# Shared expert in blocks of 128 and 48 columns over whole groups, first x1 loads moved into the attention, and other engine orders, in a decoder layer on one core

## The chip, the core and the metric

The kernel runs on one core of a Trainium2 chip. The core has TensorE (PE, matrix products into eight PSUM banks), VectorE (DVE), ScalarE (ACT), GpSimd (POOL) and SyncE (SP, here only an issuer of DMAs). Each engine works through its own instructions in order, and they meet at semaphores. Sixteen DMA engines carry every transfer, whoever issues it. The metric is the device time of the whole program in microseconds, lower is better.

## What is computed

One decoder layer over 4096 tokens (64 sequences of 64) with 256 features, all in float32: a strided self attention, an attention over 64 context rows that keeps the 54 highest scores, and a mixture of 16 routed experts (4 per token) beside one shared expert. The change touches the shared expert and the gate:

```python
x = x + _L0_attn_ref(_layernorm(x, axis=-1), ...)
x = x + _L0_xattn_ref(_layernorm(x, axis=-1), ..., ctx_2048, ctx_2048, 54)
x = x + _L0_ffn_ref(_layernorm(x, axis=-1), ...)

# in the last one: D, H, NE = 256, 176, 16
logits = jnp.einsum('ed,btd->bte', gate_w, x)
scores = jax.nn.sigmoid(logits) + gate_b
weights, indices = jax.lax.top_k(scores, TOP_K)
weights = weights / weights.sum(-1, keepdims=True)
shared_out = jax.nn.silu(x @ w1_shared) * (x @ w3_shared) @ w2_shared
h1 = jnp.einsum('btd,edc->btec', x, w1_routed)
h2 = jnp.einsum('btd,edc->btec', x, w3_routed)
h3 = jax.nn.silu(h1 * h2)
experts_out = jnp.einsum('btec,ecd->bted', h3, w2_routed)
return shared_out + routed_out
```

## The kernel before

The program has three phases with a barrier of all engines between them.

**Attention** (`attention_phase`). Four blocks of 1024 tokens, eight steps each. SP loads the inputs, stores the result rows to the DRAM scratch `x1`, and, between the loads of the first two blocks, prefetches the small weights of the next phase (`CrossInputs.load`). DVE is busy nearly all the time.

**Cross phase** (`cross_phase`). Eight groups of 512 tokens go through a software pipeline. Round i does stage s of group i - s; each engine runs the pieces of a round in the order that the table `order` lists (t is TensorE, v VectorE, s ScalarE, g GpSimd). For group n:

- stage -1 and 0: statistics and normalisation of x1 (`stA`, `rsA`, `nmA`, `xhA`), transposition (`t_a`, `t_a_ev`), queries (`at_mm`, two halves, `at_ev`) and the value side (`bp_mm`, `bp_ev`);
- stage 1: scores (`sc_mm`), their mask on VectorE (`negs`, `tops`, `masks`) with the exponential `expo` on ScalarE, the transposed probabilities (`p_t`, moved from PSUM to SBUF by ScalarE in `p_t_ev`), the product with the values (`y_mm`), the residual `x2_`, then the statistics of x2 (`stC`, `rsC` on GpSimd, `nmC`, `xhC`);
- stage 2: transposition (`t_c`, `t_c_ev`), gate (`lg_mm`, `th_`, `l_t`), routing on VectorE (`choose`, `shares`, `spread`, which needs the ranks of `rk_mm` and writes `slot`, the place of each row), and the first eight of 16 scatters of the group: `scatter(0)` and `scatter(1)` on GpSimd, each an indirect DMA of 128 rows to `xs_scratch`;
- stage 3: the other eight scatters (`scatter(2)`, `scatter(3)`), and the shared expert in two halves of 256 tokens: `sh_mm`, `g1_` (Silu), `hs_`, `ys_mm`, `xf_`.

The two normalisations are tied to GpSimd: `rsA` and `rsC` take a power of four numbers per row, and stand between the scatters of the same engine. A scatter k waits until scatter k - 2 has landed (`s_sc`, two semaphores by turns), so at most two are in flight. GpSimd's order in a round is `rsA`, four scatters, `rsC`, four scatters, and then eight of the next group, which wait for its `slot`.

The hidden width is 176. Before, it is cut in two halves of 88 (`HC`): `sh_mm` has for each half of the tokens eight products of 256 columns for 88 outputs, and the gate is a product of its own with 16 outputs. A float32 product of up to 512 columns shows as two MATMUL rows in the trace and in the counts of the profile.

At the start of the phase ScalarE issues six DMAs with the routed weights (`load_weights`, 8.65 MB on queue q10), and only then computes the coefficients `cf` for which VectorE waits before its first statistics. SP issues the first three loads of x1 (`load_x1`, 512 KB each) at the same time; for later groups it issues x1, context and output DMAs round by round.

**Experts** (`expert_phase`). 143 tiles of 128 rows are gathered from `xs_scratch`, and each result is added to the output by an indirect DMA. It starts when every engine and every scatter of the cross phase is done. The change does not touch it.

## Time and profile before

| | us |
|---|---|
| runs without profile: median (lowest, highest) of 3 | 904.76 (896.44, 906.59) |
| the profiled execution, its own time | 898.93 |
| its span, first to last instruction | 896.8 |
| attention, until the barrier | 0 to 242 |
| cross phase | 242 to 545 |
| experts | 545 to 897 |

| engine | busy us | share of the span |
|---|---|---|
| PE | 700.3 | 78% |
| DVE | 596.4 | 67% |
| POOL | 529.8 | 59% |
| ACT | 393.7 | 44% |

Busy shares are means over three phases with different limits, so they don't say what a change in one phase is worth. For that one looks at a stretch of time, asks which engine goes on without a pause or waits only for itself, and follows who waits for whom. In a timeline row the number in square brackets is the idle time of the engine just before the row, with the engine and line that ended it. Line numbers L... are those of the kernel before.

### The profile page before, as it was taken

The page shows a single profiled execution, that of the slowest core. Times are in us where ns is not written, and L with a number is a line of the kernel's source. Part 1 is how long each engine was busy: PE and PEld are TensorE (multiplying, and loading weights), DVE is VectorE, ACT ScalarE, POOL GpSimd, SP SyncE. Part 2 cuts the span into 40 slices and gives each one's busy share as a digit, 9 for nine tenths or more (in the row PEclk, how much of TensorE's full clock was granted, in tenths as well). Part 3 has the DMA queues.
Part 4 walks back from the last instruction along what each step waited for, and adds up shares of the span by engine and source line. Part 5 has one row for each costly group of instructions (what it writes and reads, how often), then busy time and mean ns, then how long its engine had stood idle before and what let it go on. Part 6 is the DMA issues. An engine that isn't in the chain of part 4 may idle for free. (4 is left out here: it accounts for less than half of the span.)

```text
span 896.8 us, 19120 instructions
## 1 busy us (share of the span) xinstructions
PE 700.3 (78%) x4330; PEld 589.3 (66%) x4330; DVE 596.4 (67%) x1833; ACT 393.7 (44%) x1051; POOL 529.8 (59%) x419
## 2 busy tenths in 40 slices
PE   0777777775405799988997754999999999898993
PEld 0556665664303567655775433899999999898993
DVE  4799999999202666554564464777777777576672
ACT  0644435352003555444542233655555555454451
POOL 0587877776300036666567671667677756764875
PEclk9988979798856999998998885999999999999997
DMA  6701111000296224433223453567677767676874
GB/s 198 248 26 41 54 35 47 29 23 19 72 302 112 71 82 150 157 128 127 104 104 122 144 187 101 95 113 132 121 126 128 125 115 126 110 131 101 132 124 54
DMA packets 86893, 99.04 MB, mean 110 GB/s; under 512 B 10401, under 2 KB 81633, under 8 KB 86753
## 3 DMA queue, kind: packets, MB, share of 16 engines
q0 software_dynamic: 26736, 37.64, 23.2%
q1 hardware_dynamic: 48971, 51.68, 19.9%
q10 hardware_dynamic: 11094, 8.65, 4.1%
q8 instruction: 39, 0.64, 0.3%
q14 instruction: 53, 0.43, 0.2%
HBM read 49.57 MB, written 52.95 MB: 114 GB/s over the span
## 5 line engine op out<-in xcount | busy, mean ns | idle before, releaser
L1412 POOL DMA_INDIRECT out_dram<-yw,xg x143 | 223.3, 1561 | 127.0 <-issue 59.1
L1008 POOL DMA_INDIRECT xs_scratch<-rows,slot x128 | 128.2, 1002 | 78.7 <-DMA xs_scratch<-rows,slot 50.1
L1305 PE MATMUL cbank<-w,stc_hi 88*128 x572 | 116.0, 295 | 1.4 <-DVE stc_lo L1377 0.5
L1305 PE MATMUL cbank<-w_hi,xtc_hi 128*128 x286 | 106.5, 372 | 0.6 <-DVE xtc_lo L1317 0.3
L1305 PEld LDWEIGHTS cbank<-w,stc_hi 88*128 88x128 f32 x572 | 90.3, 190 | 14.3 <-issue 9.2
L1305 PE MATMUL cbank<-w,xtc_hi 128*128 x286 | 94.0, 329 | 0.0
L1305 PE MATMUL cbank<-w_hi,xtc_lo 128*128 x286 | 93.6, 327 | 0.0
L455 PE MATMUL ps_o<-ident,pv 128*128 128x128 f32 x288 | 48.6, 328 | 54.9 <-ACT ot L291 50.1
L1397 DVE TENSOR_SCALAR yw<-cbank,xg 128x256 f32<-128x256 f32 x143 | 69.0, 483 | 29.1 <-PE cbank L1305 16.3
L1317 DVE TENSOR_TENSOR xtc_lo<-cbank,xtc_hi 128x256 fp32r<-128x256 f32 x143 | 60.6, 423 | 36.9 <-ACT xtc_hi L1312 26.2
L455 PEld LDWEIGHTS ps_o<-ident,pv 128*128 128x128 f32 x288 | 40.4, 170 | 63.7 <-POOL pv L256 42.8
L1305 PE MATMUL cbank<-w,stc_lo 88*128 x286 | 80.9, 283 | 0.0
L1357 ACT ACTIVATE sgc<-hh 128x176 f32<-128x176 f32 x143 | 50.1, 350 | 63.6 <-DVE hh L1351 51.7
L1345 ACT ACTIVATE h<-cbank 128x176 f32<-128x176 f32 x143 | 45.2, 316 | 71.8 <-PE cbank L1305 56.0
L1294 PE MATMUL cbank<-identb,xg 128*128 128x128 f32 x286 | 56.5, 279 | 25.5 <-DMA xg<-xs_scratch 25.5
L256 POOL TENSOR_TENSOR pv<-v_sb,pr 128x256 f32<-128x256 f32 (+7 forms) x32 | 70.0, 2187 | 6.4 <-DVE pr L423 6.4
L1351 DVE TENSOR_TENSOR hh<-cbank,h 128x176 f32<-128x176 f32 x143 | 48.5, 339 | 29.9 <-ACT h L1345 22.5
L706 POOL TENSOR_TENSOR rstd<-ve,powerb 128x4 f32<-128x4 f32 x16 | 16.5, 1028 | 75.8 <-DVE ve L700 75.6
L1312 ACT ACTIVATE xtc_hi<-cbank 128x256 fp32r<-128x256 f32 x143 | 53.5, 374 | 13.9 <-PE cbank L1294 12.8
L1377 DVE TENSOR_TENSOR stc_lo<-cbank,stc_hi 88x256 fp32r<-88x256 f32 x143 | 58.7, 410 | 1.0 <-ACT stc_hi L1372 0.9
L1305 PEld LDWEIGHTS cbank<-w_hi,xtc_hi 128*128 128x128 f32 x286 | 55.2, 193 | 2.4 <-issue 1.6
L1305 PEld LDWEIGHTS cbank<-w,xtc_hi 128*128 128x128 f32 x286 | 55.5, 194 | 0.0
(191 smaller groups left out, 1722.8 us busy)
## 6 DMA issues: line engine op xcount, KB each, us to landing
xg<-xs_scratch SPq DMA_DIRECT2D x143, 144.0 KB
x_in<-x_dram SPq DMA_DIRECT2D x32, 128.0 KB
w_hi<-ctx_t_dram SPq DMA_DIRECT2D x8, 512.0 KB, 3.6
x_scratch<-u SPq DMA_DIRECT2D x32, 128.0 KB
w_hi<-x_scratch SPq DMA_DIRECT2D x8, 512.0 KB
out_dram<-w SPq DMA_DIRECT2D x16, 256.0 KB
w<-w1r_dram ACTq DMA_DIRECT2D x2, 1408.0 KB
w<-w3r_dram ACTq DMA_DIRECT2D x2, 1408.0 KB
```

What stands on the lines that cost most here:

```text
L256: f_pv.sig(e.tensor_tensor(pv[:, p % 2, 0:w, :].rearrange("p b (h d) -> p b h d", h=H), v_sb[:, gg % 2, 0:w, :].rearrange("p b (h d) -> p ...
L455: last = e.matmul(ps_o[:, ch * P:(ch + 1) * P], pv[:, p % 2, b, ch * P:(ch + 1) * P], ident[:, :], is_transpose=True, start=b == 0, stop=b ...
L1008: nc.gpsimd.indirect_dma_start(t["xs"], bass.IndirectOffsetOnAxis(ap=slot[:, n % 2, k:k + 1].bitcast(U32), axis=0), rows[:, n % NROW, k // ...
L1294: last = nc.tensor.transpose(R[p % 2][:, ch * P:(ch + 1) * P], xg[:, p, ch * P:(ch + 1) * P], ident[:, :])
L1305: last = nc.tensor.matmul(out, stationary, moving, start=j == 0, stop=j == len(pairs) - 1)
L1312: f["t_hi"].sig(nc.scalar.activation(xt_hi[:, p % 2, :, :], x_t(p), ACT.Copy))
L1317: f["t_ev"].sig(nc.vector.tensor_tensor(xt_lo[:, p % 2, :, :], x_t(p), xt_hi[:, p % 2, :, :].bitcast(F32), ALU.subtract))
L1351: f["hh"].sig(nc.vector.tensor_tensor(hh[:, p % 2, :], R[2 + p % 2][:, 0:HID], h2[:, p % 2, :], ALU.mult))
L1357: f["sg"].sig(nc.scalar.activation(sg[:, p % 2, :], hh[:, p % 2, :], ACT.Silu))
L1377: f["st_ev"].sig(nc.vector.tensor_tensor(st_lo[:, p % 2, :, :], s_tr(p), st_hi[:, p % 2, :, :].bitcast(F32), ALU.subtract))
L1397: f["y_ev"].sig(nc.vector.tensor_scalar(yw[:, p % YB, :], R[6 + p % 2][:, 0:D], xg[:, p, bass.ds(c, 1)], None, ALU.mult))
L1412: nc.gpsimd.indirect_dma_start(t["out"], bass.IndirectOffsetOnAxis(ap=xg[:, p, ID:ID + 1].bitcast(U32), axis=0), yw[:, p % YB, :], None, c ...
```

## The change

1. **Shared expert in 128 and 48 columns, whole groups.** `sh_mm` now does all 512 tokens of a group at once with the first 128 of 176 columns: w1 into bank 2, w3 into bank 3, two products of 512 columns each. The remaining 48 columns of w1 and w3 and the 16 of the gate stand in one block `wrest` of 128 columns (48 of w3, 16 zeros, 48 of w1, 16 gate), and `rest_mm` takes the place of `lg_mm`. So the rest is computed in stage 2 (`g1r_`, `hsr_`) and the main part in stage 3 (`g1_`, `hs_`). `ys_mm` adds 128 rows of `w2s` and 48 of `w2rest`, its second half into bank 3 instead of bank 2.
2. **First x1 loads in the attention.** The three loads of x1 for groups 0 to 2 are issued by SP in the attention, after the last input loads, behind a wait for the stores of block 1 and ahead of the stores of blocks 2 and 3.
3. **Other engine orders** in `order` for TensorE, VectorE and ScalarE. GpSimd's is the same.

```diff
@@ attention_phase, SP
+            for a in range(WIN):
+                f_st[a].wait(eng, GRP - 3)
+            prefetch_rows(eng)
             with eng.Fori(GRP - 2, GRP) as g:
@@ CrossInputs
-    LOADS = 17
+    LOADS = 18
-        self.w1s, self.w3s, self.w2s = sb("w1s", [P, DC, HID]), sb("w3s", [P, DC, HID]), sb("w2s", [HC, 2, D])
+        self.w1s, self.w3s, self.wrest = (sb(n, [P, DC, P]) for n in ("w1s", "w3s", "wrest"))
+        self.w2s, self.w2rest = sb("w2s", [P, D]), sb("w2rest", [REST, D])
@@ cross_phase
             f["xhC"].wait(eng, n)
             f["rt"].wait(eng, n - 1)
+            f["hsr"].wait(eng, n - 1)
             f["tC"].sig(transpose_tiles((6, 7), rows[:, n % NROW, :, 0:D]))
...
-        def lg_mm(eng, n):
+        def rest_mm(eng, n):
             f["tC_ev"].wait(eng, n)
             for ch in range(DC):
-                last = nc.tensor.matmul(R[6][0:NE, :], gw[:, ch, :], xt3[:, n % NX3, ch, :], start=ch == 0, stop=ch == DC - 1)
+                last = nc.tensor.matmul(R[6][:, :], wrest[:, ch, :], xt3[:, n % NX3, ch, :], start=ch == 0, stop=ch == DC - 1)
...
+        def g1r_(eng, n):
+            f["lg"].wait(eng, n)
+            f["hsr"].wait(eng, n - 1)
+            f["g1r"].sig(nc.scalar.activation(g1r[:, :], R[6][GATED, :], ACT.Silu))
+
+        def hsr_(eng, n):
+            f["g1r"].wait(eng, n)
+            f["ys"].wait(eng, 2 * (n - 2) + 1)
+            f["hsr"].sig(nc.vector.tensor_tensor(hsr[:, n % 2, :], R[6][RESTS, :], g1r[:, :], ALU.mult))
...
+        def sh_mm(eng, n):
+            f["tC_ev"].wait(eng, n)
+            f["xf"].wait(eng, 2 * (n - 1) + 1)
+            for bank, w in ((2, w1s), (3, w3s)):
+                for ch in range(DC):
+                    last = nc.tensor.matmul(R[bank][:, :], w[:, ch, :], xt3[:, n % NX3, ch, :], start=ch == 0, stop=ch == DC - 1)
+            f["sh"].sig(last)
...
                 for k in range(2):
-                    for hc in range(2):
-                        last = nc.tensor.matmul(R[2][:, k * D:(k + 1) * D], hs[:, hc, k * P:(k + 1) * P],
-                                                w2s[:, hc, :], start=hc == 0, stop=hc == 1)
+                    cols = slice((2 * part + k) * P, (2 * part + k + 1) * P)
+                    o = R[2 + part][:, k * D:(k + 1) * D]
+                    nc.tensor.matmul(o, hs[:, cols], w2s[:, :], start=True, stop=False)
+                    last = nc.tensor.matmul(o, hsr[:, n % 2, cols], w2rest[:, :], start=False, stop=True)
@@ cross_phase, SP
             open_flows(eng, flows)
-            for n in range(NX1):
-                load_x1(eng, n)
             tile_table.load(eng, t)
```

What the new orders do is seen in the instructions that each engine gets. In these rows a product is `bank<-stationary or moving operands`; `w13_hi` and `w2` are the weight buffers whose space the cross phase uses for its own tiles (x1, context, transposed rows, x2).

TensorE, the first half of a full round before, from `sc_mm` (L799) over `t_a`, `t_c`, the first half of `sh_mm` (L1021), half of `at_mm`, `p_t` (L853) and the gate (L908) to `y_mm` (L871):

```order
L799 MATMUL bank4<-w13_hi 64x64 x16
L726 MATMUL bank0<-identb,w2 128x128 x4
L726 MATMUL bank1<-identb,w2 128x128 x4
L726 MATMUL bank6<-identb,rows 128x128 x4
L726 MATMUL bank7<-identb,rows 128x128 x4
L1021 MATMUL bank2<-w2,w1s 88x256 x4
L1021 MATMUL bank3<-w2,w3s 88x256 x4
L747 MATMUL bank1<-w13_hi,xwq 128x512 x2
L853 MATMUL bank5<-identb,prb 64x128 x4
L908 MATMUL bank6<-w2,gw 16x512 x2
L871 MATMUL bank4<-w13_hi,prt 128x256 x2
L871 MATMUL bank5<-w13_hi,prt 128x256 x2
```

The same stretch of the changed kernel, from `sc_mm` (L811) to the first half of `at_mm` (L759):

```order
L811 MATMUL bank4<-w13_hi 64x64 x16
L1046 MATMUL bank2<-w2,w1s 128x512 x2
L1046 MATMUL bank3<-w2,w3s 128x512 x2
L738 MATMUL bank6<-identb,rows 128x128 x4
L738 MATMUL bank7<-identb,rows 128x128 x4
L738 MATMUL bank0<-identb,w2 128x128 x4
L738 MATMUL bank1<-identb,w2 128x128 x4
L865 MATMUL bank5<-identb,prb 64x128 x4
L883 MATMUL bank4<-w13_hi,prt 128x256 x2
L883 MATMUL bank5<-w13_hi,prt 128x256 x2
L923 MATMUL bank6<-w2,wrest 128x512 x2
L759 MATMUL bank1<-w13_hi,xwq 128x512 x2
```

The whole shared part stands behind `sc_mm`, and between `p_t` (L865) and `y_mm` (L883) nothing stands any more; in rounds 1 and 2, which have no shared part yet, between `sc_mm` and `p_t` only the transpositions are left.

TensorE, the second half of a full round before: the first `ys_mm` (L1050), the other half of `at_mm`, `l_t`, the second half of `sh_mm`, `bp_mm` (L778), and behind it `rk_mm` and the second `ys_mm`:

```order
L1050 MATMUL bank2<-w2s,hs 128x256 x4
L747 MATMUL bank0<-w13_hi,xwq 128x512 x2
L921 MATMUL bank7<-identb,th 128x16 x4
L1021 MATMUL bank2<-w2,w1s 88x256 x4
L1021 MATMUL bank3<-w2,w3s 88x256 x4
L778 MATMUL bank0<-xwo,w13_hi 128x256 x4
L778 MATMUL bank1<-xwo,w13_hi 128x256 x4
```

The same of the changed kernel:

```order
L936 MATMUL bank7<-identb,th 128x32 x4
L1069 MATMUL bank2<-w2s,hs 128x256
L1070 MATMUL bank2<-w2rest,hsr 128x256
L1069 MATMUL bank2<-w2s,hs 128x256
L1070 MATMUL bank2<-w2rest,hsr 128x256
L759 MATMUL bank0<-w13_hi,xwq 128x512 x2
L790 MATMUL bank0<-xwo,w13_hi 128x256 x4
L790 MATMUL bank1<-xwo,w13_hi 128x256 x4
L1069 MATMUL bank3<-w2s,hs 128x256
L1070 MATMUL bank3<-w2rest,hsr 128x256
L1069 MATMUL bank3<-w2s,hs 128x256
L1070 MATMUL bank3<-w2rest,hsr 128x256
```

The second half of `at_mm` (L759) now stands directly ahead of `bp_mm` (L790), with nothing between; the second `ys_mm` stands ahead of `rk_mm`.

VectorE behind `x2_` (L885), before: the first `xf_` (L1064), `nmA` (L711), `stC` (L692 to L700), then `choose` from L942 on:

```order
L885 SCALAR_TENSOR_TENSOR w2<-bank5,rdenb,w13_hi 128x256 x2
L1064 TENSOR_TENSOR w2<-bank2,w2 128x512
L711 SCALAR_TENSOR_TENSOR nmb<-mvb,rstd 128x4
L692 BN_STATS st<-w2 128x6 x4
L697 BN_AGGR mvb<-st 128x2 x4
L700 TENSOR_SCALAR ve<-mvb 128x4
L942 SCALAR_TENSOR_TENSOR sg<-bank7,gb_half 128x64
```

The same of the changed kernel:

```order
L897 SCALAR_TENSOR_TENSOR w2<-bank5,rdenb,w13_hi 128x256 x2
L1059 TENSOR_TENSOR hs<-bank3,g1 128x512
L704 BN_STATS st<-w2 128x6 x4
L709 BN_AGGR mvb<-st 128x2 x4
L712 TENSOR_SCALAR ve<-mvb 128x4
L1083 TENSOR_TENSOR w2<-bank2,w2 128x512
L970 SCALAR_TENSOR_TENSOR sg<-bank7,gb_half 128x64
```

`stC`, whose last result `ve` GpSimd's `rsC` waits for, no longer stands behind the first `xf_` and behind `nmA`; both `nmA` and `nmC` now come after `choose`.

## Rows read from the trace of the kernel before

**Rows 1.** Windows by stage: PE, PEld, DVE, ACT, POOL busy, PEclk, DMA share, GB/s.

```profile
242.20:270.70 28.50, 0.00 (x0) 0.00 (x0) 1.62 (x11) 0.30 (x2) 0.76 (x3) 0.51 1.02 280
270.70:326.66 55.96, 41.02 (x254) 26.75 (x254) 28.24 (x151) 25.49 (x51) 6.04 (x6) 0.89 0.38 89
326.66:542.14 215.48, 181.97 (x986) 126.08 (x986) 120.93 (x525) 89.49 (x153) 138.65 (x138) 0.91 0.38 133
542.14:896.80 354.66, 323.42 (x2288) 306.84 (x2288) 233.15 (x588) 185.08 (x588) 223.25 (x143) 0.95 0.68 115
```

**Rows 2.** POOL's group of scatters, 326 to 543: busy, mean ns, idle before by releaser.

```profile
L1008 POOL DMA_INDIRECT xs_scratch<-rows,slot x128 | 128.2, 1002 | 78.7 <-DMA xs_scratch<-rows,slot 50.1 <-issue 17.8 <-DVE slot L983 10.7
```

**Rows 3.** POOL's timeline: start us, us, instruction, idle before it.

```profile
326.66 1.19 POOL L1008 DMA_INDIRECT xs_scratch<-rows,slot  x1 [4.73 <-DVE slot L983]
...
380.80 0.96 POOL L1008 DMA_INDIRECT xs_scratch<-rows,slot  x1 [2.79 <-DMA xs_scratch<-rows,slot]
...
430.43 1.04 POOL L706 TENSOR_TENSOR rstd<-ve,powerb 128x4 f32<-128x4 f32 x1 [2.64 <-DVE ve L700]
...
439.70 0.96 POOL L1008 DMA_INDIRECT xs_scratch<-rows,slot  x1 [3.02 <-DVE slot L983]
...
465.79 0.96 POOL L1008 DMA_INDIRECT xs_scratch<-rows,slot  x1 [2.97 <-DVE slot L983]
...
541.18 0.95 POOL L1008 DMA_INDIRECT xs_scratch<-rows,slot  x1 [0.48 <-DMA xs_scratch<-rows,slot]
```

**Rows 4.** Windows of PE alone, rounds 4, 6 and 7, from one sc_mm to the next.

```profile
351.05:378.29 27.24, 25.58 (x155) 1.00 0.45 153
...
406.50:438.71 32.21, 28.53 (x155) 0.89 0.31 113
438.71:464.75 26.04, 25.48 (x156) 1.00 0.31 111
```

**Rows 5.** ACT's timeline at the start of the cross phase.

```profile
244.74 13.05 ACTq L1100 DMA_DIRECT2D w<-w3r_dram  x2
257.82 10.53 ACTq L1103 DMA_DIRECT2D w<-w2r_dram  x2
268.40 0.20 ACT L1192 ACTIVATE cf<-scal 128x1 f32<-128x1 f32 x1 [32.20 <-issue]
```

**Rows 6.** Windows of all engines in that wait; the last two numbers are DMA share, GB/s.

```profile
244.00:268.40 24.40, 0.00 (x0) 0.00 (x0) 0.00 (x0) 0.00 (x1) 0.00 (x0) 0.50 1.10 311
246.00:256.00 10.00, 0.00 (x0) 0.00 (x0) 0.00 (x0) 0.00 (x0) 0.00 (x0) 0.50 1.11 349
256.00:266.00 10.00, 0.00 (x0) 0.00 (x0) 0.00 (x0) 0.00 (x0) 0.00 (x0) 0.50 1.18 304
```

**Rows 7.** PE's timeline: round 1 from p_t on, then the shared part in round 4.

```profile
296.29 0.62 PE L853 MATMUL bank<-identb,prb 128*64 128x128 f32 x4 [0.16 <-DVE prb L845]
297.78 1.99 PE L871 MATMUL bank<-w_hi,prt 128*128 128x256 f32 x8 [0.87 <-ACT prt L861]
...
302.91 3.72 PE L778 MATMUL bank<-xwo,w_hi 128*128 128x256 f32 x16 [1.42 <-ACT w_hi L758]
306.56 1.20 PE L799 MATMUL bank<-w_hi 128*64 128x64 f32 x32
...
353.99 1.89 PE L1021 MATMUL bank<-w,w1s 128*88 128x256 f32 x8
...
357.44 1.88 PE L747 MATMUL bank<-w_hi,xwq 128*128 128x512 f32 x4
```

**Rows 8.** Timeline of ACT and PE in round 6.

```profile
419.87 0.78 ACT L861 ACTIVATE prt<-bank 64x256 f32<-64x256 f32 x2 [2.34 <-remote]
420.70 3.78 PE L871 MATMUL bank<-w_hi,prt 128*128 128x256 f32 x8 [3.68 <-ACT prt L861]
424.27 3.21 PE L1050 MATMUL bank<-w2s,hs 88*128 88x256 f32 x8
```

**Rows 9.** Timeline of DVE at the end of the cross phase.

```profile
532.11 7.29 DVE L1134 TENSOR_TENSOR w<-w,w_hi 128x704 fp32r<-128x704 f32 x9
```

More of the change, by code:

```diff
@@ L619, in cross_phase @@
         G = GT * D
[L620 removed]
+        x1 = pre.x1
         bp = place[:, 3 * G:5 * G].rearrange("p (g t d) -> p g t d", g=2, t=GT)
@@ L1138, in cross_phase @@
         order = dict(
-            t=[(1, sc_mm), (0, t_a), (2, t_c), (3, sh_mm(0)), (0, at_mm(1)), (1, p_t), (2, lg_mm), (1, y_mm), (3, ys_mm(0)),
-               (0, at_mm(0)), (2, l_t), (3, sh_mm(1)), (0, bp_mm), (2, rk_mm), (3, ys_mm(1)), (2, table_mm)],
-            v=[(1, negs), (1, tops), (1, masks), (-1, stA), (3, split_lo(range(0, 4))), (3, hs_(0)), (1, x2_),
-               (3, split_lo(range(4, 7))), (3, xf_(0)), (-1, nmA), (1, stC), (2, choose), (1, nmC), (3, hs_(1)), (2, shares),
-               (2, spread), (3, xf_(1)), (2, table), (3, split_lo(range(7, NE)))],
-            s=[(0, t_a_ev), (1, expo), (2, t_c_ev), (3, g1_(0)), (1, p_t_ev), (2, th_), (0, at_ev), (-1, xhA), (3, g1_(1)),
-               (0, bp_ev), (1, xhC), (2, split_hi(range(0, 7))), (3, split_hi(range(7, NE)))],
+            t=[(1, sc_mm), (3, sh_mm), (2, t_c), (0, t_a), (1, p_t), (1, y_mm), (2, rest_mm), (0, at_mm(1)), (2, l_t),
+               (3, ys_mm(0)), (0, at_mm(0)), (0, bp_mm), (3, ys_mm(1)), (2, rk_mm), (2, table_mm)],
+            v=[(1, negs), (1, tops), (1, masks), (-1, stA), (3, split_lo(range(0, 4))), (1, x2_), (3, hs_),
+               (3, split_lo(range(4, 7))), (1, stC), (3, xf_(0)), (2, choose), (-1, nmA), (1, nmC), (2, shares), (3, xf_(1)),
+               (2, spread), (2, hsr_), (2, table), (3, split_lo(range(7, NE)))],
+            s=[(1, expo), (2, t_c_ev), (1, p_t_ev), (0, t_a_ev), (3, g1_), (2, th_), (0, at_ev), (2, g1r_), (-1, xhA),
+               (1, xhC), (0, bp_ev), (2, split_hi(range(0, 7))), (3, split_hi(range(7, NE)))],
             g=[(-1, rsA), (3, scatter(2)), (1, rsC), (3, scatter(3)), (2, scatter(0)), (2, scatter(1))])
```

90 lines of the change are left out of this document (42 added, 48 removed).

## The prediction

> **What bounds the kernel now.** I read the windows by stage first, since the page's busy shares mix three phases. In [rows 1] the attention before 242 and the expert phase behind 542 run the same instructions after the change; what can move is 242 to 542. It has three pieces: 28.50 us in which hardly anything computes, 55.96 us until the first scatter, and 215.48 us of scatters.
>
> In that third piece TensorE looks like the limit: 181.97 us busy of 215.48 in [rows 1], and in [rows 4] rounds 4 to 7 show 25.48 to 28.53 us of work in 26.04 to 32.21. GpSimd looks idle, 138.65 us. But the groups of GpSimd in [rows 2] say otherwise. Of the 78.7 us that it stands before its 128 scatters, 50.1 end with a landed scatter (its own, two earlier), 17.8 with nothing but its own issue, and only 10.7 with VectorE's `slot`; of these 4.73 lie before the first scatter, as [rows 3] show. So from 326.66 to 542.14 GpSimd waits for another engine three times, for 2.64, 3.02 and 2.97 us [rows 3], 8.63 in all. From 465.79 to the end, 76 us, it waits for none. A group of scatters with no wait for others: from 439.70 to 465.79 it is 26.09, less the 2.97, so 23.1 us; where bulk loads delay a landing, as at 380.80 with 2.79, it is longer. The other 207 us are a chain of its own that TensorE's work doesn't enter. The reader should see that a 90% busy TensorE is here only the second limit, and that at most 8.63 us of its work can be collected behind the first scatter.
>
> **The start (x1 loads moved).** ScalarE computes `cf` at 268.40 after 32.20 us in which it waited for nothing but its own issue: its last four DMA issues take 13.05 and 10.53 us [rows 5], because the queue accepts them only as fast as it drains. [rows 6] have the DMA engines full: 349 GB/s in 246 to 256 and 304 in 256 to 266. In the first of these the three x1 loads, 1.57 MB, share the engines. From 244 to 268.4, 24.4 us at 311 GB/s are 7.6 MB; less the x1 bytes that is 6.0 MB of weights ahead of ScalarE's release. At 304 GB/s they take 19.8 us from 244, at 349 GB/s 17.2: release at 263.8 or 261.2 instead of 268.4, a gain of 4.6 to 7.2 us. Were the queue limited by its number of descriptors rather than by bytes, it would be less (x1 has 1536 of some 11,000 ahead of the release, an eighth of 24 us: 3). I take 4.6, nearest to the rate of the stretch in which the weights were alone. The DMA page of the Trainium skill (DMA: Bandwidth & Descriptors, Queues, rings and completion order) says that each DMA engine goes round its queues packet by packet, by which x1's packets are paid for by the weights'; the fall of the rate only when x1 is through agrees.
>
> In the attention the three issues stand ahead of the stores of block 2. They cost SP two or three us of waiting and 1.57 MB at 349 GB/s, 4.5 us, at a time when the attention moves little; the stored tile is needed about two steps of some 6 us later. I cost this at nothing; if that cover is gone it is at most the 4.5.
>
> **Rounds 1 and 2 (orders).** Here nothing of stage 3 runs, and only lost cover shows. `p_t` starts when the mask is done, 296.29, as before; `y_mm` at 297.78 as before [rows 7]. Before, half of `at_mm` was done ahead of `p_t`; now both halves come after `y_mm`. One half takes about 1.8 us (two product pairs of 512 columns, the row at 357.44), so `bp_mm` and round 2 start 1.8 us later. In round 2 before, a gate product, a half of `at_mm` and a second transposition lay under the mask and the eviction of `prt`. Now: `p_t` 5.8 us after `sc_mm`, `y_mm` 1.49 later, itself 1.8, `rest_mm` 1.8, half of `at_mm` 1.8, `l_t` 0.4, the other half with the wait for `at_ev` 3.3 (from 299.6 to 302.91, of which 1.42 is the wait), `bp_mm` 3.65 (302.91 to 306.56), ranks 0.45: 20.5 us, where the round took 17.6. That is 2.9 later. Sum 4.7 us later to the first `slot`. With the 4.6 of the start the first scatter comes at 326.66 - 4.6 + 4.7 = 326.8: nothing gained.
>
> **Full rounds.** One of the two `sh_mm` pieces goes, 353.99 to 357.44, 3.45 us [rows 7]. The wider gate block costs the same as the narrow one, since both are two products of 512 columns; `ys_mm` keeps its eight of 256, VectorE and ScalarE keep the number and length of their operations (one Silu and one product of 48 rows in place of the second half). TensorE's work falls from 25.48 [rows 4] to 22.0. But the order gives some of it back: 0.9 us between `p_t` and `y_mm`, 1.42 ahead of `bp_mm`. So a round takes 24.4 us if nothing else holds it, against 26.04. GpSimd's group takes 23.1 without bulk traffic and some 27 with it. In rounds 3 to 5, with x1 and context loads, GpSimd stays the limit and nothing is gained. In rounds 6 and 7 the three waits are at stake. The 2.64 (`ve`) goes, because `stC` no longer stands behind `xf_`. The 3.02 and 2.97 (`slot`) go as far as TensorE keeps ahead: 24.4 against 23.1 leaves 1.3 a round, less the lead won in rounds 3 to 5; I leave 1 us. So 8.63 - 1 = 7.6 us.
>
> **Tail.** VectorE's last weight splits end at 539.4 [rows 9], 2.7 us before the last scatter. They must come forward too, and they do: the second Silu of the last round, ahead of ScalarE's second batch, is gone, some 8 us.
>
> **Sum.** 0.1 later to the first scatter, 7.6 off the chain: 7.5 us. The profiled execution, 898.93, would become 891.4; its time lies 5.8 below the median of the three runs. On the median: 904.76 - 7.5 = 897.3. About 1% is what a measurement of this kernel can tell from no change.
>
> **Rivals.**
>
> *A. Orders overlap better than I count (chance 0.33).* The lost cover in rounds 1 and 2 turns out at 2 us, the start gives its 7.2, the whole 8.63 is collected: 7.2 - 2 + 8.6 = 13.8 us, time 891. For it: my 4.7 assumes each wait in full. Against: the rows of the two waits, 1.42 and 0.87, stand there already in round 1, where the order is like the new one.
>
> *B. The clock falls in the new pauses (0.12).* In round 6 TensorE was idle for 3.68 us and then ran `y_mm` in 3.78 and `ys_mm` in 3.21 us [rows 8], against 1.99 and 1.89 else; the granted clock of that round is 0.89 [rows 4], some of it at the lower level, 1.2 GHz. Now TensorE has 3 us less work in rounds that GpSimd paces at 27, so a pause of that size may come each round. It costs 3.1 us each time. Where GpSimd paces, this is hidden; it decides from the point at which 24.4 + 3.1 exceeds 27, in rounds 6 and 7: the gain of 7.6 falls to about 2. Time 903. The page TensorE: Matmul & The Clock Gate (HAM oscillation) of the Trainium skill warns of such pauses between bursts, which speaks against a change that takes work off a paced TensorE; the trace has one such pause in a full round.
>
> *C. Slower: the mask comes late (0.08).* VectorE now ends a round with `spread` and `hsr_` behind `nmC`, which waits for `rsC` on GpSimd, and nothing but the shared part and two transpositions lies on TensorE between `sc_mm` and `p_t`. If VectorE starts the mask late, TensorE stands ahead of `p_t`, and `y_mm`, `rest_mm` and `bp_mm` behind it are late too. It decides from 27 - 24.4 = 2.6 us a round on. At 5 us a round takes 29.4: 2.4 longer in each of rounds 3 to 5, and in rounds 6 and 7 about what the two take now (32.21 and 26.04 [rows 4], 29.1 on average, so 0.3 each). 0.1 + 7.2 + 0.6 = 8 us, time 913. Against it: before, `xf_` stood where `hsr_` stands now, with the same length.
>
> *D. Nothing gained at all (0.07).* ScalarE's stall in round 6, 2.34 us and more ended by nothing on the core [rows 8], comes again elsewhere, and POOL waits as before: 904.
>
> **How the numbers follow.** My forecast has 0.40, A 0.33, B 0.12, C 0.08, D 0.07. Faster by over 1% (below 895.7) holds A and about a quarter of my own case, 0.43; within 1% the rest of it with B and D and a part of C, 0.49; slower 0.08. The range takes in A with the profile's scatter of runs and B and D: 886 to 907.
>
> **What would show it.** Right: `cf` at about 264; the first scatter at 325 to 328; round 2 longer than 19 us with a pause ahead of `p_t`; rounds 4 and 5 still near 27 us; no wait of POOL for `ve`, and less than 2 us for `slot` behind the first; the last scatter near 534.5; the expert phase unchanged at 354 us. Wrong: a first scatter before 323 (A), full rounds with clock under 1.00 and more than 27 us (B), `cf` still at 268 (C), or groups of scatters without bulk traffic that differ from 23.1 us.

## The result and the profile after

The changed kernel took 905.71 us (median), the kernel before 899.45 us beside it: ratio 1.0068, interval 1.0042 to 1.0093. The forecast was 897.3, with 0.43 on faster, 0.49 on no change that can be told and 0.08 on slower. The time lies inside the range 886 to 907, but the sign was wrong, and the place in the range says little: the forecast was 7.5 us off a median of three runs, 904.76, and against the 899.45 measured beside the changed kernel it would have read 892.0. Timed twice more, the same changed kernel gave 0.9968 (0.9938 to 0.9998) and 1.0108 (1.0074 to 1.0142), so its ratio moves by up to 1.4% from one occasion to another, and even its sign isn't settled; why is part of what follows. The clear finding is that the 7.5 us never came.

The windows by stage of the profile after (from, to, length, then PE, PEld, DVE, ACT and POOL busy with counts, PEclk, DMA share, GB/s): the wait for ScalarE, the stretch to the first `sc_mm`, rounds 1 and 2, three of the full rounds, all scatters, the expert phase.

```profile
243.09:264.72 21.63, 0.00 (x0) 0.00 (x0) 0.00 (x0) 0.00 (x1) 0.76 (x3) 0.50 1.05 281
264.72:287.69 22.97, 11.90 (x32) 6.94 (x32) 5.79 (x30) 6.67 (x14) 2.01 (x2) 0.63 0.64 114
287.69:307.51 19.82, 14.01 (x77) 9.53 (x76) 9.64 (x51) 8.31 (x17) 2.01 (x2) 0.83 0.16 53
307.51:329.64 22.13, 17.11 (x108) 11.45 (x107) 12.61 (x71) 10.29 (x20) 2.01 (x2) 0.92 0.14 48
329.64:356.15 26.51, 23.82 (x133) 14.44 (x130) 15.87 (x79) 16.47 (x30) 15.91 (x16) 1.00 0.41 133
356.15:386.83 30.68, 25.35 (x134) 15.54 (x131) 16.31 (x81) 15.24 (x26) 19.49 (x20) 0.94 0.42 142
414.05:440.43 26.38, 23.82 (x134) 14.44 (x131) 16.28 (x81) 13.96 (x25) 18.46 (x19) 1.00 0.33 118
332.17:545.36 213.19, 160.31 (x800) 92.62 (x798) 119.57 (x525) 91.36 (x153) 138.16 (x138) 0.92 0.39 134
545.36:902.50 357.14, 323.82 (x2288) 305.15 (x2288) 232.66 (x588) 185.98 (x588) 223.24 (x143) 0.96 0.67 114
```

Against [rows 1]: the stretch from the barrier to the first scatter is 84.5 us there (242.20 to 326.66) and 89.1 here, although ScalarE is released after 21.63 us. Rounds 1 and 2 together take 41.95 us with the clock at 0.83 and 0.92; before they took 33.62 at 1.00 (16.05 up to 306.56 [rows 7], and 17.57). A full round holds 23.8 us of TensorE's work, not the 22.0 forecast ([rows 4]: 25.5). The scatters take 213.19 us, 2.3 less than before; 7.6 less was forecast. The expert phase, whose instructions are the same, is 2.5 longer in this pair. Over all profiles of this study it lies between 354 and 361, with no clear relation to the edit, so I count that as scatter; nothing here tests it.

ScalarE's timeline after, up to its release (start, length, instruction, idle before it):

```profile
245.61 8.69 ACTq L1119 DMA_DIRECT2D w<-w3r_dram  x2
264.72 0.20 ACT L1209 ACTIVATE cf<-scal 128x1 f32<-128x1 f32 x1 [28.26 <-issue]
```

GpSimd's group of scatters after, 320 to 546:

```profile
L1036 POOL DMA_INDIRECT xs_scratch<-rows,slot x128 | 127.7, 998 | 84.3 <-DMA xs_scratch<-rows,slot 43.8 <-DVE slot L1011 20.9 <-issue 19.6
```

The issue of w3 takes 8.69 us where it took 13.05 [rows 5]. But the waits for `slot` have doubled against [rows 2], to 20.9: 9.48 of them lie before the first scatter, 11.4 behind it, where less than 2 was forecast.

Round 1 after in windows of 2 us of TensorE alone (its busy time, PEclk, DMA share, GB/s):

```profile
290.00:292.00 2.00, 0.09 (x1) 0.97 0.22 90
292.00:294.00 2.00, 0.52 (x3) 0.50 0.00 0
294.00:296.00 2.00, 1.14 (x4) 0.50 0.00 0
296.00:298.00 2.00, 2.00 (x6) 0.50 0.01 4
298.00:300.00 2.00, 2.00 (x6) 0.83 0.00 0
```

TensorE's timeline there:

```profile
293.48 1.06 PE L865 MATMUL bank<-identb,prb 128*64 128x128 f32 x4 [3.39 <-DVE prb L857]
295.41 3.60 PE L883 MATMUL bank<-w_hi,prt 128*128 128x256 f32 x8 [0.86 <-ACT prt L873]
298.85 3.60 PE L759 MATMUL bank<-w_hi,xwq 128*128 128x512 f32 x8
303.86 3.72 PE L790 MATMUL bank<-xwo,w_hi 128*128 128x256 f32 x16 [1.42 <-ACT w_hi L770]
```

With only the scores and one transposition to do ahead of the mask, TensorE pauses 3.39 us; the granted clock falls to the lower level, 0.50 or 1.2 GHz, and `y_mm` takes 3.60 us instead of 1.99 [rows 7]. The starts of these rows split the 3.8 us that round 1 loses. From `p_t` to `y_mm` and on to `at_mm` it is 1.93 and 3.44 us, where it was 1.49 and 1.84: 2.05 for the clock. From `at_mm` to `bp_mm` it is 5.01 instead of 3.29: 1.7 for the half of `at_mm` that lost its cover.

And where the full round's missing 1.8 us is: TensorE's timeline in one `ys_mm` after, then the timeline of its weight loads (PEld) there.

```profile
428.09 0.70 PE L1069 MATMUL bank<-w2s,hs 128*128 128x256 f32 x2
428.72 0.70 PE L1070 MATMUL bank<-w2rest,hsr 48*128 48x256 f32 x2
429.35 0.70 PE L1069 MATMUL bank<-w2s,hs 128*128 128x256 f32 x2
```

```profile
428.72 0.29 PEld L1070 LDWEIGHTS bank<-w2rest,hsr 48*128 48x128 f32 x2 [0.33 <-issue]
429.35 0.30 PEld L1069 LDWEIGHTS bank<-w2s,hs 128*128 128x128 f32 x2 [0.33 <-issue]
```

The weight loads around one `ys_mm` in the kernel before, with those of `y_mm` ahead of it and of `at_mm` behind it:

```profile
361.51 1.59 PEld L871 LDWEIGHTS bank<-w_hi,prt 128*128 128x128 f32 x8 [0.85 <-issue]
363.13 1.70 PEld L1050 LDWEIGHTS bank<-w2s,hs 88*128 88x128 f32 x8
364.86 0.41 PEld L747 LDWEIGHTS bank<-w_hi,xwq 128*128 128x128 f32 x2
```

The products alternate between 128 and 48 rows of contraction. One starts every 0.63 us. Before, with 88 rows throughout, the loads ran without a gap and one product started every 0.43 us. Even the step from 128 rows in `y_mm` to 88 and back to 128 in `at_mm` shows no gap. Now a load waits 0.33 us wherever the height changes between 128 and 48 rows. Eight products in a round at 0.2 us are 1.6 us.

### The profile page after: what moved, and what is told of

It is laid out like the page before. It is cut to its first block and busy times, and to the rows that moved or that the text cites. A ratio compares the mean times of both kernels' runs of the same rounds, so it can differ in the third digit from the quotient of the medians.

```text
span 902.5 us, 18750 instructions
## 1 busy us (share of the span) xinstructions
PE 682.7 (76%) x4138; PEld 555.0 (61%) x4138; DVE 596.3 (66%) x1833; ACT 398.6 (44%) x1053; POOL 528.3 (59%) x419
## 5 line engine op out<-in xcount | busy, mean ns | idle before, releaser
L1374 ACT ACTIVATE sgc<-hh 128x176 f32<-128x176 f32 x143 | 50.1, 350 | 64.1 <-DVE hh L1368 51.9
L290 ACT ACTIVATE pr<-sc 128x16 f32<-128x16 f32 (+7 forms) x32 | 8.4, 263 | 107.8 <-DVE sc L391 107.8
```

The lines of the kernel that those rows point to most:

```text
L1374: f["sg"].sig(nc.scalar.activation(sg[:, p % 2, :], hh[:, p % 2, :], ACT.Silu))
```

## Experiments

Each ratio is to the kernel before, run on the same chip beside the experiment; kernels that shared these runs are said to be of one occasion.

**The start alone.** The kernel before with the three x1 loads issued in the attention (the diff's `prefetch_rows` and `load_x1` parts), nothing else.

> The kernel before with part 2 of the change alone: the first three x1 loads are issued inside the attention. Theory 1 (the start gains as reckoned, the loss of the whole change lies in rounds 1 and 2 and in the ys products): the coefficients come 4.6 us after a shorter wait, the first scatter 3.5 to 4.6 us earlier than the 326.7 of before, the whole 0.4 to 0.5% faster. Rival (moving the loads costs something in the attention or later, for the barrier came 0.9 us later and the expert phase took 2.5 us more in the changed kernel): the barrier is again 0.9 us or more later than 242.2, the expert phase again about 357 us, and the whole is not faster.

888.99 us, ratio 0.9964 (0.9949 to 0.9979).

```profile
244.74 8.44 ACTq L1109 DMA_DIRECT2D w<-w3r_dram  x2
263.25 0.20 ACT L1199 ACTIVATE cf<-scal 128x1 f32<-128x1 f32 x1 [27.64 <-issue]
```

The issue of w3 starts at the same time as before [rows 5], 244.74, and takes 8.44 us instead of 13.05. The first scatter comes at 322.61, 4.05 earlier. The attention pays nothing. This part was right and is worth 3 to 4 us, a little less in the ratio than expected.

**The pauses of rounds 1 and 2.** The changed kernel with six products whose result nobody reads, ahead of `p_t` in these two rounds:

```
+ if n < 2:
+     for j in range(6):
+         nc.tensor.matmul(R[2][:, 0:D], wq[:, j % DC, 0:P], wo[:, j % DC, :], ...)
```

> The changed kernel with six extra products of 256 columns ahead of p_t in rounds 1 and 2, into an unused bank; their result is not used. Theory 1 (the pauses of 3.39 and 2.72 us ahead of p_t let the clock fall, which makes rounds 1 and 2 longer by 3.6 us than the lost cover alone): clock 1.00 in both rounds, y_mm 1.99 us instead of 3.60 and 2.89, round 1 about 18 us instead of 19.8, round 2 about 20.5 instead of 22.1, the first scatter 3.4 us earlier. Rival (the clock has nothing to do with the pauses): the rows after p_t stay slow and the rounds as long.

891.49 us, ratio 1.0000 (0.9985 to 1.0015). Windows of its rounds 1 and 2, same columns as above:

```profile
285.76:305.22 19.46, 16.25 (x89) 11.53 (x88) 9.63 (x51) 8.31 (x17) 2.02 (x2) 0.91 0.17 54
305.22:325.66 20.44, 18.00 (x119) 12.73 (x119) 12.54 (x71) 10.29 (x20) 2.02 (x2) 1.00 0.16 53
```

Round 2 keeps clock 1.00 and takes 20.44 us, where the prediction had summed 20.5 from lost cover alone. The padded version of the next experiment, without filler and of the same occasion, took 22.13 there. So lost cover is 2.9 us of round 2's loss and the clock the other 1.7. Round 1 still loses its clock, against my expectation, with pauses of 0.80 and 0.87 us left on either side of `p_t`: the filler cures one round of two.

**The 48-row products.** First the same products with `hsr` and `w2rest` filled up with zeros to 128 rows. Then the changed kernel with the pair turned in every second block, 128, 48, 48, 128.

```
- self.w2s, self.w2rest = sb("w2s", [P, D]), sb("w2rest", [REST, D])
+ self.w2s, self.w2rest = sb("w2s", [P, D]), sb("w2rest", [P, D])
- hsr = sb("hsr", [REST, 2, GTOK])
+ hsr = sb("hsr", [P, 2, GTOK])      # zeroed once; hsr_ writes rows 0 to 47
```

> The changed kernel with the 48 rows of hsr and w2rest padded to 128 by rows of zeros, so that every product of ys_mm has the full height. Theory 1 (a product that follows one of another height can't load its stationary operand during it, 0.63 against 0.43 us a product): the products take 0.43 us again, a full round falls by 1.6 us from 26.4 to about 24.8, POOL's waits for slot fall from 11.5 us behind the first scatter to 4 to 7, the whole is 0.3 to 0.6% faster than the changed kernel, at a ratio to before of 1.001 to 1.004. Rival (they are slow since two stationary operands of different tiles, or the wider hs, are read): the products stay at 0.63 us and the ratio at 1.007.

> The changed kernel, where of the two products for each block of tokens the order is turned in every second block: 128, 48, 48, 128 rows instead of 128, 48, 128, 48. Work and results are the same. Theory 1 (it is the change of height from one product to the next that costs 0.2 us, 0.63 us for such a product against 0.43 us): the second product of 48 rows starts 0.43 us after the first, and the load of its weights with no idle time ahead; the two that follow a change still take 0.63. Full rounds hold 0.4 to 0.8 us less of TensorE's work than 23.8. Rival (a product of 48 rows takes 0.63 us wherever it stands, or an unaligned height does): 0.63 us behind the first 48-row product too, and 23.8 us a round. Time: one look, 0 to 2 us under the changed kernel, not told apart from it.

Padded: 894.68 us, ratio 1.0026 (1.0003 to 1.0049). Mirrored: one run of 899.17. Two full rounds of the padded kernel (windows), then two of its weight loads in one `ys_mm`:

```profile
352.73:377.73 25.00, 22.34 (x133) 15.11 (x130) 15.62 (x76) 12.38 (x21) 14.66 (x16) 1.00 0.43 144
377.73:406.73 29.00, 24.08 (x133) 16.05 (x130) 16.52 (x82) 14.19 (x25) 19.04 (x21) 0.94 0.42 139
```

```profile
396.19 0.41 PEld L1070 LDWEIGHTS bank<-w2rest,hsr 128*128 128x128 f32 x2
```

One `ys_mm` of the mirrored kernel, TensorE's products and then their loads:

```profile
406.56 1.13 PE L1071 MATMUL bank<-w2rest,hsr 48*128 48x256 f32 x4
407.62 0.70 PE L1071 MATMUL bank<-w2s,hs 128*128 128x256 f32 x2
```

```profile
406.56 0.73 PEld L1071 LDWEIGHTS bank<-w2rest,hsr 48*128 48x128 f32 x4 [0.33 <-issue]
407.62 0.30 PEld L1071 LDWEIGHTS bank<-w2s,hs 128*128 128x128 f32 x2 [0.33 <-issue]
```

At one height the gap is gone, a product takes 0.43 us and a full round holds 22.34 us, near the 22.0 forecast. In the mirrored order the two products of 48 rows, one behind the other, start 1.06 us before the next: 0.63 and 0.43. Within `ys_mm` the gap stands at each change between 128 and 48 rows and nowhere else, and its 23.13 us of work in a round lie between the two others. More arithmetic is cheaper here than such a change. Of the 1.8 us that the forecast missed in a round this is 1.5 (23.82 against 22.34); the other 0.3 I can't place. At what height between 48 and 88 the cost begins no run shows.

But the chain of scatters isn't shorter for it. TensorE's 1.5 us a round become pauses: the padded kernel's scatters take 205.6 us from first to last, those of the filler version of the same occasion 204.8. In one of its rounds shown above (29.00 us) TensorE paused 1.70 and then 0.92 us, and `y_mm` ran at the lower clock, 3.01 us. That is the prediction's rival B, and GpSimd's chain as the limit. The changed kernel itself was not timed on this occasion, so what padding alone does to the time is open.

**Which order costs.** The changed kernel with all three orders of before (twice), with TensorE's and ScalarE's only, with VectorE's only; and the changed kernel itself, twice more. The core of the diff is TensorE's row:

```
- t=[(1, sc_mm), (3, sh_mm), (2, t_c), (0, t_a), (1, p_t), (1, y_mm), (2, rest_mm), (0, at_mm(1)), ...
+ t=[(1, sc_mm), (0, t_a), (2, t_c), (3, sh_mm), (0, at_mm(1)), (1, p_t), (2, rest_mm), (1, y_mm), (0, at_mm(0)), ...
```

> The changed kernel, with the orders of before on TensorE, VectorE and ScalarE as far as its pieces allow: the second transposition and one half of the output projection stand between the scores and the transposition of the mask again. Theory 1 (lost cover and the clock that falls in the pause cost 8.4 us in rounds 1 and 2): round 1 takes 16.1 us at clock 1.00 instead of 19.8 at 0.83, round 2 about 17.7 instead of 22.1, and the first scatter comes at 323 to 325 instead of 332.2. The alternating products of 128 and 48 rows stay, so full rounds hold 23.8 us of TensorE's work. GpSimd's chain from the first scatter to the last stays at 213 to 216 us. Time: that of before less about 4, ratio 0.993 to 0.998. Rival (the new orders pay in full rounds, and the old ones take it back): the first scatter at 324 too, but the chain of scatters is 5 us or more longer than in the changed kernel, and the ratio is 1.002 or more.

> The changed kernel with TensorE's and ScalarE's orders of before and VectorE's new one. With all three orders of before it took 886.3 us (ratio 0.985), with all three new ones 0.7% more than before. Theory 1 (it is TensorE's order that costs: nothing left between sc_mm and p_t, and the wait ahead of bp_mm): the first scatter at 322 to 325 instead of 332.2, rounds 1 and 2 at clock 1.00 and 16 and 18 us, ratio 0.983 to 0.990. Rival (VectorE's order costs, because the mask or the residual comes late behind hsr_ and stC): rounds of 26 to 27 us stay, ratio 0.998 or more, even where the first scatter is early.

> The changed kernel with VectorE's order of before alone (hs_ ahead of x2_, xf_ behind choose, as in the run with all three orders of before); TensorE and ScalarE keep the new ones. Theory 1 (TensorE's order costs): nothing is won, the first scatter stays at 330 to 333, the pauses of 3.4 and 2.7 us ahead of p_t stay, ratio 1.003 to 1.012. Rival (VectorE's order costs): ratio 0.99 or less.

> The changed kernel with all three orders of before, again, which took 886.3, ratio 0.985, where before takes 900. Theory 1 by the run with two of the three orders (0.996 where before takes 892): 0.990 to 0.997 on a chip without late starts, since 0.7 to 1% of the 1.5% was that the kernel before has late starts and this one none; 0.983 to 0.988 on the chip with them. Rival (VectorE's order of before gives the rest): 0.985 on both.

> The changed kernel itself, beside the others of this call on one chip. Theory 1 (orders and 48-row products cost as much as start and saved products gain): on a chip where no late starts show (the kernel before takes 892 there) ratio 1.000 to 1.006, first scatter at 329 to 332, no wait of ScalarE or VectorE that nothing on the core ends. On a chip where they show (the kernel before takes 900): 1.004 to 1.010. Rival (the slower result was a matter of the late starts alone): on a chip without them the change is faster, 0.995 or less.

> The changed kernel itself, a third time. Theory 1 (start and saved products against orders and 48-row products, a draw): ratio 0.996 to 1.004, with late starts or without. Rival (the first result is the true one): 1.005 or more.

| version | time | before beside it | ratio (interval) | first scatter |
|---|---|---|---|---|
| all orders of before | 886.29 | 900.25 | 0.985 (0.9815 to 0.9886) | 321.52 |
| the same again | 888.81 | 901.08 | 0.9854 (0.9809 to 0.9899) | 321.57 |
| TensorE's and ScalarE's | 889.88 | 892.79 | 0.996 (0.9937 to 0.9983) | 322.70 |
| VectorE's | 892.89 | 892.79 | 1.0007 (0.9987 to 1.0028) | 329.44 |
| the change itself, second | 898.51 | 901.08 | 0.9968 (0.9938 to 0.9998) | 332.09 |
| third | 909.20 | 899.56 | 1.0108 (1.0074 to 1.0142) | 332.74 |

Windows of rounds 1 and 2 with the orders of before (the second such run), and then of the changed kernel of the same occasion:

```profile
285.64:301.70 16.06, 12.21 (x78) 8.11 (x77) 9.64 (x51) 6.56 (x13) 2.01 (x2) 1.00 0.20 66
301.70:318.97 17.27, 15.26 (x108) 10.54 (x107) 12.23 (x70) 10.18 (x19) 2.01 (x2) 1.00 0.19 62
```

```profile
285.50:306.25 20.75, 14.95 (x77) 9.86 (x76) 9.63 (x51) 8.30 (x17) 2.01 (x2) 0.84 0.16 51
306.25:329.56 23.31, 18.28 (x107) 12.23 (x107) 12.61 (x71) 10.29 (x20) 2.01 (x2) 0.85 0.13 46
```

The orders cost 10.7 us in these two rounds, and 9.7 us of the time on one occasion (898.51 against 888.81). It is TensorE's order (with ScalarE's, which was turned together with it): with these two of before, rounds 1 and 2 take 16.05 and 17.26 us, with VectorE's alone 19.46 and 22.13. With all orders of before, the rest of the change is 1.5% faster than the kernel before on both occasions where that takes 900, and 1.1% faster than the changed kernel on the one that has both. The near relative with two orders gave 0.4% where before takes 892, and there it is only 3.0 us ahead of the version with VectorE's alone: the first scatter comes 6.7 us earlier, but the last only 3.0 (530.48 against 533.47). So the price of the orders depends on the occasion too.

Five of the six ratios came out other than expected: 0.985 for 0.993 to 0.998 (all orders, first time), 0.996 for 0.983 to 0.990 (TensorE's and ScalarE's), 1.0007 for 1.003 to 1.012 (VectorE's), and for the change itself 0.9968 for 1.004 to 1.010 and 1.0108 for 0.996 to 1.004. The changed kernel as it stands was never timed on an occasion where before takes 892.

One full round of the version with two orders of before:

```profile
348.06:372.41 24.35, 23.44 (x134) 14.51 (x131) 16.39 (x80) 13.84 (x25) 14.81 (x17) 1.00 0.43 144
```

So the change does have a shorter round, about the 24.4 forecast, but with the old order of TensorE, in which hardly a wait is left ahead of `y_mm` and `bp_mm`.

**Four scatters in flight instead of two.** One semaphore per scatter modulo four, in the kernel before, in the changed one, and in two combinations:

```
- s_sc = [sem(f"fb_sc{k}") for k in range(2)]
+ s_sc = [sem(f"fb_sc{k}") for k in range(4)]
```

> The kernel before with four semaphores in place of two for the scatters, so that scatter k waits for scatter k - 4 and up to four are in flight. Theory 1 (GpSimd's own chain sets the cross phase of the kernel before): the waits of POOL on landed scatters, 50.1 us, nearly vanish, and the time between the first and the last scatter falls from 215.5 us to what TensorE's rounds and the tail need, some 195 to 205 us; the whole is 1 to 2% faster. Rival (the scatters are limited by the DMA engines or by TensorE's rounds): POOL waits as long on other things and the whole stays within 0.3%.

> The kernel before with the x1 loads inside the attention and four scatters in flight; no other part of the change. Theory 1: the two gains add, 0.4% of the first and 1.8% of the second, so ratio 0.976 to 0.982, with full rounds of 25.4 us. Rival (the late starts are a matter of how many scatters are in flight): stalls as in the changed kernel with four, ratio above 0.99.

> The changed kernel with up to four scatters in flight instead of two. Before with the same edit took 876.5 us, ratio 0.982, with full rounds of 25.4 us at TensorE 100% busy. Theory 1 (TensorE's round of the changed kernel is 23.8 us of work and 2.3 us of waits ahead of y_mm and bp_mm, 26.2 to 26.5 in all, and only GpSimd's chain hid that it is longer than before's): full rounds of 26.3 us, first scatter at 330 to 332, last at about 528; time about 886, ratio 0.991 to 0.996, so 10 us slower than before with four in flight. Rival (the changed kernel has the shorter round, as forecast, and only rounds 1 and 2 cost): full rounds of 24.5 us, last scatter at about 515, time 873 or less, ratio 0.98 or below.

> The changed kernel with the cover of before in its orders, with the 48 rows of the second product padded with zeros to 128 rows, and four scatters in flight. Theory 1: rounds 1 and 2 take 16.1 and 17.7 us, full rounds hold 22.3 us of TensorE's work and take 22.5 to 24 us; first scatter at 323 to 325, the last at 505 to 512; time 862 to 872, ratio 0.967 to 0.977, faster than before with four in flight (0.982). Rival (GpSimd's own work of about 18 us a group and VectorE's round, or the bulk loads, set the pace with four in flight, so TensorE's saving is not collected): first scatter at 324, but a chain of 191 us as in before with four in flight, last scatter at 515, time 872 or more.

> The changed kernel with four scatters in flight, and 64 small unused products (128 instructions of TensorE with their loads) put ahead of its first product of this phase, at a time when it waits. Without them this kernel took 919.7 us, ratio 1.018: in five rounds ScalarE's prt started 2.15 us and VectorE's residual 2.9 us after the records show TensorE's last product of them done, waits that nothing on the core ended, and in each of these rounds a transfer of 16 KB of TensorE's instructions lands within 0.3 us of the start of prt. Such a transfer comes once in some 265 instructions of TensorE, and a round of the changed kernel has about 265 (before about 310), so it meets the same place of the round each time. Theory 3 (the signal is late where TensorE's next block of instructions is being loaded): 128 instructions further on, the late starts move to another place of the round or go, and the time changes by 5 us or more, most likely to 895 to 910. Rival (four scatters in flight slow this kernel by themselves): 915 to 925, with the late starts at prt and the residual as before.

Before with four: 876.5 us, 0.9819 (0.9798 to 0.9841). With x1 early too: 870.45, 0.9742 (0.9724 to 0.9761). The changed kernel: 919.68, 1.0179 (1.0126 to 1.0233). With cover and padding: 894.68, 0.995 (0.9922 to 0.9978). The changed kernel with 64 unused products ahead: 880.89, 0.9863 (0.984 to 0.9886). The third and fourth missed my expectations (886, and 862 to 872) by 34 and 23 us; both are of the occasion where before takes 900, and the late starts described below fill their profiles. The version with cover and padding was not timed on any other. GpSimd's group of scatters in the kernel before with four in flight:

```profile
L1008 POOL DMA_INDIRECT xs_scratch<-rows,slot x128 | 129.2, 1010 | 53.7 <-issue 35.8 <-DVE slot L983 17.9
```

A window of one full round in the kernel before with x1 early and four in flight, and of one in the changed kernel with the 64 products, of one occasion:

```profile
345.30:370.71 25.41, 25.41 (x156) 18.10 (x155) 16.64 (x80) 13.83 (x26) 17.59 (x18) 1.00 0.47 165
```

```profile
349.82:376.26 26.44, 23.83 (x134) 14.45 (x131) 16.28 (x81) 13.98 (x25) 17.58 (x18) 1.00 0.42 143
```

No wait for a landed scatter is left, where [rows 2] had 50.1 us, and the scatters take 191 us instead of 215 (with x1 early, and no late starts in either profile, 191.7 with four against 208.9 with two): GpSimd's chain was the limit before, as the prediction said. Once it is gone TensorE is, and the kernel before then has the **shorter** round, 25.41 against 26.44. The changed one has 23.82 of work and waits 0.31 for the mask, 0.87 for `prt` and 1.44 ahead of `bp_mm`, in all 26.4. The forecast had 24.4: the waits were right (0.9 and 1.42), the work was 1.8 short.

**Late starts.** The spread between occasions is left. On one of the occasions where before takes 900: the changed kernel with four, without and with the 64 products; on another, the fastest version again:

> The changed kernel with four scatters in flight, again, now on the same chip as the version with 128 instructions of TensorE ahead (which took 880.9, ratio 0.986, on a chip where the kernel before takes 892; this one took 919.7, ratio 1.018, on a chip where it takes 900). Theory 3 (late starts come from the place of TensorE's blocks of instructions): ratio 1.01 to 1.02 on any chip, late starts at prt in five rounds. Rival (the chip makes them): on a chip where before takes 892 there are none, and the ratio is 0.984 to 0.988; on the other chip both versions with four have them.

> The same with the 128 instructions ahead, again. Theory 3: 0.984 to 0.990 on any chip, without late starts. Rival (the chip makes them): as the version without these instructions on the same chip, within 0.003.

> The kernel before with the x1 loads inside the attention and four scatters in flight, again; it gave 0.974 where the kernel before takes 892 and no late starts showed. Where before takes 892: 0.972 to 0.977. Where it takes 900 and late starts show: theory 4 (they strike where an engine waits for TensorE's signal, and in this kernel TensorE is 100% busy, so few of them cost) 0.97 to 0.98, full rounds of 25.4 to 26; rival (four scatters in flight make them cost, as in the changed kernel with four, 1.018 to 1.024): above 1.0.

927.29 us, 1.0241 (1.0176 to 1.0305); 921.37 us, 1.0185 (1.0131 to 1.024); and 944.89 us, 1.0497 (1.045 to 1.0545), where that same kernel had taken 870.45 before. ScalarE's timeline at `prt` in the kernel with the 64 products, on the first occasion and then on the second:

```profile
383.81 0.78 ACT L873 ACTIVATE prt<-bank 64x256 f32<-64x256 f32 x2 [0.73 <-PE bank L865]
```

```profile
400.35 0.78 ACT L873 ACTIVATE prt<-bank 64x256 f32<-64x256 f32 x2 [2.86 <-remote]
```

ScalarE's timeline in the fastest version, on the first occasion and then on the second, with TensorE's `y_mm` behind it:

```profile
378.07 0.59 ACT L1041 ACTIVATE g<-bank 88x512 f32<-88x512 f32 x1
379.45 0.78 ACT L870 ACTIVATE prt<-bank 64x256 f32<-64x256 f32 x2 [0.79 <-PE bank L862]
```

```profile
399.25 0.59 ACT L1041 ACTIVATE g<-bank 88x512 f32<-88x512 f32 x1 [6.30 <-remote]
400.76 0.78 ACT L870 ACTIVATE prt<-bank 64x256 f32<-64x256 f32 x2 [0.92 <-remote]
```

```profile
401.59 3.46 PE L880 MATMUL bank<-w_hi,prt 128*128 128x256 f32 x8 [8.00 <-ACT prt L870]
```

"remote" is a wait that nothing recorded on the core ended. TensorE had finished `g`'s input at 388.96, ten microseconds ahead. On the two occasions where the kernel before takes 892 to 893, no profile has such a wait between the first and the last full round. On the others, where it takes 899 to 901, most have. The profile before of the first sections has them too, not only in round 6:

```profile
389.54 0.78 ACT L861 ACTIVATE prt<-bank 64x256 f32<-64x256 f32 x2 [3.29 <-remote]
484.37 0.59 ACT L1032 ACTIVATE g<-bank 88x512 f32<-88x512 f32 x1 [10.52 <-remote]
```

With four scatters in flight they come in nearly every full round, and the same kernel is 40 to 75 us apart between two occasions (880.89 to 921.37, 870.45 to 944.89). My theory 3, that they stand where a block of TensorE's instructions is loaded, fell: the 128 instructions ahead made no lasting difference, and on the second occasion the late `prt` comes at the same place of the round (400.35, 430.53, 460.76) although those blocks now land elsewhere (384 to 385, 415 to 416, 445 to 446). What makes them is open. It isn't the chip alone: one chip took 892 and 893 for the kernel before on two occasions and 901 on a third. I could not choose the occasion, and nothing here separates the machine from its neighbours' traffic.

## Why the prediction was wrong

1. **What bounds it: right.** GpSimd's chain behind the first scatter is the limit, shown by the runs with four in flight (191 us without its waits) and by padding, which left the chain as long (205.6 against 204.8 us).
2. **Start: right.** 4.6 us forecast; the wait for `cf` went from 26.19 (242.21 to 268.40) to 21.63, 4.6 less, and x1 alone brought 3 to 4. The packet-by-packet sharing that the prediction took from the Trainium skill (DMA: Bandwidth & Descriptors, Queues, rings and completion order) fits: the weights gained what x1's bytes had cost (1.57 MB at 349 GB/s are 4.5 us). The `cf` at 264.72 was forecast as "about 264".
3. **Rounds 1 and 2: the step that failed first.** I summed 1.8 and 2.9 us of lost cover; measured 3.8 and 4.6. The terms were right (1.7 by the rows of round 1, and a round 2 of 20.44 against 20.5 with the clock held); what they left out is the clock, 2.05 and 1.7 us. I had rival B's falling clock only in rounds 6 and 7, and named a pause ahead of `p_t` in round 2 as a sign without pricing it. The first scatter came at 332.17 instead of 326.8: 3.6 from these two rounds, 0.9 from the barrier (243.09) and 0.9 from the stretch to `sc_mm` (22.97 against 22.11). The page TensorE: Matmul & The Clock Gate (HAM oscillation) of the Trainium skill warns that a wait between two bursts of products throttles TensorE again and the next burst starts slow. The trace agrees, with a pause of 3.39 us and a `y_mm` of 3.60, in a place where I had not applied it.
4. **Full rounds: a mis-sized term.** "`ys_mm` keeps its eight of 256" at the same cost: it costs 1.5 to 1.6 us more. 22.0 should have been 23.8, and the round 26.4, longer than the 25.4 of before. I took the number and width of the products for the whole price. What it cost with two scatters in flight no run shows (item 5).
5. **Chain: -7.6 forecast, -2.3 measured: the second step that failed.** The wait for `ve` went, as forecast. The `slot` waits did not, they grew to 11.4 us behind the first scatter. I had taken three waits of GpSimd, 8.63 us, for a steady property of the engine orders, and each us of them for a us of the chain. Neither holds. GpSimd's scatters with x1 alone, in the changed kernel with filler, and with VectorE's order of before, all three from profiles without late starts:

```profile
L1017 POOL DMA_INDIRECT xs_scratch<-rows,slot x128 | 127.8, 999 | 76.2 <-DMA xs_scratch<-rows,slot 57.7 <-issue 13.7 <-DVE slot L992 4.7
L1039 POOL DMA_INDIRECT xs_scratch<-rows,slot x128 | 126.4, 988 | 77.4 <-DMA xs_scratch<-rows,slot 56.9 <-issue 11.8 <-DVE slot L1014 8.7
L1036 POOL DMA_INDIRECT xs_scratch<-rows,slot x128 | 127.0, 992 | 76.9 <-DMA xs_scratch<-rows,slot 49.0 <-DVE slot L1011 15.5 <-issue 12.3
```

With x1 alone all 4.7 us of `slot` lie before the first scatter and there is no wait for `ve` behind it: nothing was there to collect. In the profile before, the three waits (430.43, 439.70, 465.79) stand behind the late `prt` of 419.87. The second version has its 8.7 before the first scatter too. The third waits 6.0 us for `slot` behind it, but 49.0 instead of 56.9 for landings, and its chain is no longer: 204.0 us from first to last, against 204.8 with filler and 208.9 with x1 alone. Nor did rounds of 26.4 us lengthen the chain there: the padded version has 25.0 in a free round and needs 205.6. Why the changed versions lie 3 to 5 us below 208.9 is open. On the occasion of the result there was one late `prt` (3.61 us of TensorE's waiting, a round of 30.68 us at clock 0.94), and the waits for `slot` of 3.90, 1.53, 2.94 and 3.09 us stand behind it. Rounds of 26.4 against GpSimd's groups of 26 to 27 leave little to win that back; whether rounds of 24.4 would have, no run shows. This is rival D, to which I had given 0.07 on the strength of one round, although the trace before has such waits of 2.08 to 10.52 us at 389.54, 416.94, 448.48 and 484.37 as well.
6. **Tail and expert phase.** The last scatter started at 544.40, not near 534.5, as items 3 and 5 have it. The expert phase took 357.14 us instead of the 354 named as unchanged; see the scatter above.

The sum by the measured terms: -4.6 for the start, +1.8 ahead of round 1, +8.3 in rounds 1 and 2, -2.3 on the chain, +2.5 in the expert phase: 5.7 us, as between the two profiled spans (902.5 and 896.8), and 6.3 between the medians. Against the forecast of -7.5 that is 13.2 us: 5.4 up to the first scatter, 5.3 on the chain, 2.5 in the expert phase.

## What to carry to other kernels

Work that is moved off a waiting engine's path also takes away what kept it busy: price each new pause twice, as lost cover and as what the next products cost at the lower clock, and above all in the first rounds, where the pipeline is not yet full. Counting products and columns isn't enough for TensorE: look at the height of neighbouring products too. Here 128 beside 48 rows cost 0.2 us a product and 128 beside 88 nothing, and padding to one height took 1.5 us off TensorE's round, though not off the chain that set the time. Before adding up another engine's waits as a gain, look whether they stand behind a single late event, and whether the engine would wait for something else in their place. Time a candidate on more than one occasion: the version that won 2.6% on one occasion lost 5% on another. With two scatters in flight the kernel before moved only between 892 and 901.
